# Attention's output normalisation split between ScalarE and VectorE, with the residual addition moved to the next turn

## What is computed

```python
x = x + 0.5 * ffn(layernorm(x))
x = x + attn(layernorm(x))
x = x + 0.5 * ffn(layernorm(x))

def attn(x):                       # windows of 128 tokens
    q, k, v = x @ Wq.T + bq, x @ Wk.T + bk, x @ Wv.T + bv
    scores = q @ k.T / sqrt(128)   # per window; only the 32 largest of each row are kept
    out = leaky_relu(softmax(top32(scores)) @ v, 0.01)
    r = out + x
    mu, var = mean(r), var(r)      # over the 128 features
    return (r - mu) / sqrt(var + 1e-5) * gamma + beta

def ffn(x):                        # router picks 2 of 8 experts per token, and a shared expert
    n = layernorm(x) * ln_gamma + ln_beta
    gates = softmax(top2(softmax(n @ router_w.T)))
    return sum(gate_e * swiglu_e(n)) + swiglu_shared(n)   # 384 wide per expert, 128 shared
```

## Time and profile before

| | us |
|---|---|
| median of 3 runs | 587.57 |
| lowest and highest | 584.46, 588.54 |
| the profiled execution | 590.26 |
| its span, first to last instruction | 588.5 |
| mean granted TensorE clock, share of full speed | 0.96 |

### The profile page before, as it was taken

One profiled execution on the slowest core, in us unless ns is written; L12 is line 12 of the kernel. 1 busy time (PEld: TensorE's weight loads), 2 busy tenths in 40 slices (PEclk: granted clock), 3 DMA queues, 4 the chain that ended last, 5 costly groups with the idle time before them and its releaser, 6 DMA issues.

```text
span 588.5 us, 14528 instructions
## 1 busy us (share of the span) xinstructions
PE 500.2 (85%) x3928; PEld 457.6 (78%) x3928; DVE 386.5 (66%) x1716; ACT 330.6 (56%) x792; POOL 332.8 (57%) x491
## 2 busy tenths in 40 slices
PE   2588999889999989998967399996899899899881
PEld 2466989889999989997964279784899889899780
DVE  5568774722558898877796978989885423222664
ACT  3376655665468576566753376763755446655330
POOL 2274856775566674365563506663667765565542
PEclk9999999999999999999987789996999999999986
DMA  6945787776776544783411174422658667777983
GB/s 180 319 105 177 229 239 247 225 244 228 257 258 235 195 171 160 248 283 123 156 43 58 42 250 159 167 99 98 219 202 233 239 219 245 258 257 235 321 274 110
DMA packets 88013, 117.83 MB, mean 200 GB/s; under 512 B 11848, under 2 KB 60880, under 8 KB 87936
## 3 DMA queue, kind: packets, MB, share of 16 engines
q1 hardware_dynamic: 76208, 96.75, 49.8%
q0 software_dynamic: 9312, 19.16, 9.4%
q10 hardware_dynamic: 2416, 0.99, 0.9%
HBM read 26.57 MB, written 26.19 MB: 90 GB/s over the span
## 4 chain that ended last, share of the span: by engine, by line
PE 51%; SPq 12%; ACT 11%; issue 8%; DVE 7%; DMA 7%; POOL 3%; ACTq 1%; POOLq 0%; DVEq 0%
PE ps_y L729 12%; PE ps_g L715 11%; PE ps_h L720 5%; PE ps_u L720 5%; SPq L440 4%; DMA xin<-rows 3%; SPq L483 3%; PE w L629 3%; SPq L478 3%; ACT zz L848 2%; PE ps_x L710 2%; PE w L659 2%; POOL rows L1552 2%; DMA yg<-results 2%; PE w L678 2%
## 5 line engine op out<-in xcount | busy, mean ns | idle before, releaser
L1569 POOL DMA_INDIRECT results<-raw_gu,idx x163 | 164.5, 1009 | 155.6 <-ACT raw_gu L928 112.8
L1552 POOL DMA_INDIRECT rows<-zz,s_idx x128 | 126.5, 988 | 65.0 <-issue 30.0
L729 PE MATMUL ps_y<-dn_t,raw_gu 128*128 x978 | 140.6, 281 | 10.2 <-ACT raw_gu L928 8.6
L715 PE MATMUL ps_g<-x_t,raw_dn 128*128 128x128 f32 x978 | 138.4, 278 | 0.0
L729 PEld LDWEIGHTS ps_y<-dn_t,raw_gu 128*128 128x128 f32 x978 | 124.3, 194 | 15.8 <-issue 15.4
L715 PEld LDWEIGHTS ps_g<-x_t,raw_dn 128*128 128x128 f32 x978 | 123.8, 194 | 3.0 <-issue 2.7
L928 ACT COPY raw_gu<-ps_y 128x128 f32<-128x128 f32 x163 | 43.0, 264 | 105.3 <-PE ps_y L729 104.1
L922 ACT ACTIVATE sil<-ps_g 128x384 f32<-128x384 f32 x163 | 80.1, 492 | 21.3 <-PE ps_g L715 20.1
L919 ACT ACTIVATE x_t<-ps_x,bf_c,gf_c 128x128 f32<-128x128 f32 x163 | 75.4, 463 | 18.3 <-PE ps_x L710 17.4
L1379 DVE TENSOR_TENSOR raw_gu<-sil,ps_u 128x384 f32<-128x384 f32 x82 | 45.1, 550 | 57.4 <-PE ps_u L720 45.2
L1379 DVE TENSOR_TENSOR raw_gu<-sil,ps_h 128x384 f32<-128x384 f32 x81 | 44.6, 551 | 50.8 <-PE ps_h L720 38.5
(11 more groups left out here) (168 smaller groups left out, 735.3 us busy)
## 6 DMA issues: line engine op xcount, KB each, us to landing
raw_dn<-gu_t SPq DMA_DIRECT2D x163, 384.0 KB
xin<-rows SPq DMA_DIRECT2D x163, 64.5 KB
yg<-results SPq DMA_DIRECT2D x15, 512.0 KB, 5.1
results<-raw_gu,idx POOLq DMA_INDIRECT x163
rows<-pads SPq DMA_DIRECT2D x40, 64.5 KB
rows<-pads SPq DMA_DIRECT2D x5, 451.5 KB, 6.0
rows<-zz,s_idx POOLq DMA_INDIRECT x128, 2.9
out<-xres SPq DMA_DIRECT2D x7, 256.0 KB, 2.8
```

Of the source, the lines that this page charges most:

```text
L715: t = pe.matmul(ps_g[k][:, c, :], ws[:, k4, c * P:(c + 1) * P], x_t[:, k, :], start=True, stop=True)
L729: t = pe.matmul(ps_y[:, 0, :], h_t[:, k4, c * P:(c + 1) * P], dn[:, bass.ds(off + c * D, D)], start=(c == 0), stop=(c == FC - 1))
L1552: pool.indirect_dma_start(xs, bass.IndirectOffsetOnAxis(s_idx[n][:, c, k:k + 1], 0), zz[n][:, k, c, :], None).then_inc(scat[n], 16)
L1569: pool.indirect_dma_start(yt, bass.IndirectOffsetOnAxis(idx[:, ky:ky + 1], 0), yb[:, ky, :], None).then_inc(yst[ky], 16)
```

## The change

ScalarE gets a new function `norm_r`: four activations per turn (one per tile) that write rn = rr * rstd + nmr, with rstd and nmr as per-partition pointers; it stands behind the exponentials in turns T1 to T7, and ahead of the shared Silu in T8. VectorE makes nmr for this normalisation with one more small `centre` at place 24. VectorE's `scaled` is removed, and `attended` becomes two operations on all four tiles at once, 128x512: rn = rn * gamma, and xres = xres + rn. They stand at the beginning of the next turn (T2 to T9), after the preparation of step p and in front of `stats_route`. A new buffer `rn` is added. The numbers in `WEAVE` are new.

```diff
@@ -112,22 +112,22 @@
 
 WEAVE = {
     "sp": """
...
     "pe": """
...
     "act": """
...
     "dve": """
...
     "pool": """
...
 }
 
 
@@ -282,6 +282,7 @@
         pr_t = sb("pr_t", [P, TB, P])
         o = sb("o", [P, TB, D])
         rr = sb("rr", [P, TB, D])
+        rn = sb("rn", [P, TB, D])
 
 
         gt = sb("gt", [P, NT, NE])
@@ -338,8 +339,8 @@
         s_ps, sc_sb, tk, nm_done, ex_done, pr_done, ri_done, prT_ps, prT_sb, o_ps = (
             sem(n) for n in ("s_ps", "sc_sb", "tk", "nm_done", "ex_done", "pr_done", "ri_done", "prT_ps", "prT_sb", "o_ps"))
         o_sb = sem("o_sb")
-        lr_done, rr_done, rg_done, xb_done, x2_done = (
-            sem(n) for n in ("lr_done", "rr_done", "rg_done", "xb_done", "x2_done"))
+        lr_done, rr_done, rn_done, rg_done, xb_done, x2_done = (
+            sem(n) for n in ("lr_done", "rr_done", "rn_done", "rg_done", "xb_done", "x2_done"))
         out_st, spare = sem("out_st"), sem("spare")
         passed = {e: sem(f"passed_{n}") for e, n in (
             (nc.vector.engine, "dve"), (nc.gpsimd.engine, "pool"), (nc.sync.engine, "sp"))}
@@ -353,7 +354,7 @@
 
         CREDITS = [(xT_ps, 4), (idx_cp, 4), (xT_sb, 3), (g_ps, 5), (u_ps, 4), (sil_done, 4), (h_done, 5),
                    (y_ps, 8), (y_sb, 6), (shh, 1), (xr_done, 1), (prT_sb, 1), (pr_done, TB), (ex_done, TB),
-                   (nm_done, 1), (o_ps, 1), (o_sb, 1), (v_sb, 1), (x2_done, TB), (cb, 2 * 3)]
+                   (nm_done, 1), (o_ps, 1), (o_sb, 1), (v_sb, 1), (x2_done, 1), (rn_done, TB), (cb, 2 * 3)]
 
         ctx.enter_context(nc.allow_low_precision(reason="rows' numbers are whole and below 2**24, exact in float32"))
         block = ctx.enter_context(nc.Block())
@@ -890,6 +891,14 @@
                 act.wait_ge(ex_done, (a + 1) * TB)
                 act.copy(sc[:], w0[:]).then_inc(sc_sb, 1)
 
+            def norm_r(A):
+
+                act.wait_ge(nw2, A * (N_NW + 1) + (N_NW + 1))
+                for k in range(TB):
+                    act.activation(rn[:, k, :], rr[:, k, :], ACT.Identity,
+                                   bias=nmr[:, AFTER_AT + k:AFTER_AT + k + 1], scale=rstd[:, AFTER_AT + k:AFTER_AT + k + 1]).then_inc(rn_done, 1)
+                    turn()
+
             def shared(R):
                 act.wait_ge(shG, R + 1)
                 act.activation(sg[:], w0[:].rearrange("p t d -> p (t d)"), ACT.Silu).then_inc(sg_done, 1)
@@ -992,11 +1001,15 @@
                     turn()
                     keys(p)
                     turn()
+                if a is None and A is not None:
+                    norm_r(A)
                 if J is not None:
                     shared(STEPS + J)
                     turn()
                 if a is not None:
                     exps(a)
+                if a is not None and A is not None:
+                    norm_r(A)
             gates_of_layer(1)
             turn.rest()
             for B in range(FIRST[-1], FIRST[-1] + YB):
@@ -1047,7 +1060,7 @@
                 stats(lambda k: rr[:, k, :], AFTER_AT, bn2, ag2, A * TB, turn)
 
             def stats_route(R, A, tile):
-                dve.wait_ge(x2_done, A * TB + 2 * TB)
+                dve.wait_ge(x2_done, A + 2)
                 stats(lambda k: res(tile, k), ROUTE_AT, bn3, ag3, R * TB, turn)
 
             def newton(n, chain, at, lo, mid, hi):
@@ -1088,7 +1101,12 @@
 
             def norms_after(n, A):
 
-                newton(n, nw2, A * N_NW, AFTER_AT, AFTER_AT + TB, AFTER_AT + TB)
+                if n == 0:
+                    dve.wait_ge(ag2, A * TB + TB)
+                if n < N_NORM:
+                    newton(n, nw2, A * (N_NW + 1), AFTER_AT, AFTER_AT + TB, AFTER_AT + TB)
+                else:
+                    centre(AFTER_AT, AFTER_AT + TB, nw2)
 
             def first_stats(R):
 
@@ -1315,21 +1333,16 @@
                 dve.tensor_tensor(xr, xr, wide(ba_b), ALU.add).then_inc(xb_done, 1)
                 turn()
 
-            def scaled(k, A):
-
-                if k == 0:
-                    dve.wait_ge(ag2, A * TB + TB)
-                dve.scalar_tensor_tensor(rr[:, k, :], rr[:, k, :], mv[:, AFTER_AT + k, 0:1], ga_b[:], ALU.subtract, ALU.mult).then_inc(rg_done, 1)
-                turn()
-
-            def attended(k, A):
-
-                dve.wait_ge(rg_done, A * TB + k + 1)
-                if k == 0:
-                    dve.wait_ge(nw2, A * N_NW + N_NW)
+            def attended(m, A):
+
+                if m == 0:
+                    dve.wait_ge(rn_done, A * TB + 2 * TB)
+                    dve.tensor_tensor(rn[:], rn[:], wide(ga_b), ALU.mult).then_inc(rg_done, 1)
+                else:
+                    dve.wait_ge(rg_done, A + 1)
                     dve.wait_ge(xb_done, A + 1)
-                dve.scalar_tensor_tensor(res(A * TB, k), rr[:, k, :], rstd[:, AFTER_AT + k:AFTER_AT + k + 1], res(A * TB, k),
-                                         ALU.mult, ALU.add).then_inc(x2_done, 1)
+                    xr = xres[:, A * TB:A * TB + TB, :]
+                    dve.tensor_tensor(xr, xr, rn[:], ALU.add).then_inc(x2_done, 1)
                 turn()
 
             def values(a):
@@ -1461,6 +1474,8 @@
                 R, rt = (None, None) if Jr is None else (STEPS + Jr, Jr * TB)
                 after = AFTER if a is not None else AFTER_LATE
                 if R is not None:
+                    attended(0, Jr)
+                    attended(1, Jr)
                     stats_route(R, Jr, rt)
                 if A is not None:
                     biased(A)
@@ -1475,12 +1490,8 @@
                         leaky(A, A % XRING)
                     if m == after + 1 and A is not None:
                         stats_after(A)
-                    if after + 2 <= m < after + 2 + TB and A is not None:
-                        scaled(m - (after + 2), A)
-                    if after + 2 <= m < after + 2 + N_NORM and A is not None:
+                    if after + 2 <= m <= after + 2 + N_NORM and A is not None:
                         norms_after(m - (after + 2), A)
-                    if after + 2 + N_NORM <= m < after + 2 + N_NORM + TB and A is not None:
-                        attended(m - (after + 2 + N_NORM), A)
                     if PICKS <= m <= PICKS + N_PICK and R is not None:
                         pick(m - PICKS, R, rt)
                     if m == (SHARED if a is not None else SHARED_LATE) and R is not None:
```

24 lines of the change are left out of this document (12 added, 12 removed).

## The result

| | before | after |
|---|---|---|
| median, us (runs) | 586.44 (4) | 592.98 (4) |
| lowest to highest, us | 584.46 to 588.54 | 590.36 to 596.97 |
| profiled execution, us (span) | 590.26 (588.5) | 591.35 (589.5) |

The account below looks back on a forecast made before the run. Bounds: VectorE's work from a turn's beginning to nmr in two holes, TensorE in full stretches. 0.8 + 1.1 + 1.2 - 0.6 - 0.6 = +1.9 us on 587.57 gives 589.5 us; 8-of-10 range 582.5 to 594.5.

Parts of the forecast that it names:

- The holes (T4, T5, T7: +0.8, +1.1, +1.2): Stretches 298 to 341 and 387 to 409.3 us, where TensorE lacks work: the pair in front of nmr lengthens them.
- The signs: nmr of T5 and T7 1 to 1.5 us later from s_idx; TensorE's idle time before L608 grows by as much.
- T8, T9 and the rest ... -0.6.: TensorE has blocks there, lacking 2.75 us in 440 to 480: -0.6 us, bounds -1.5 and +1.
- ScalarE. ... I take 0.: Four activations, 1.6 us per turn, nearly fit idle time behind T3's exponentials: 0, bounds 0 and +0.5 in seven turns.
- ScalarE delays the Silus: Rival, T1 to T7: rn's activations delay the first block work behind the exponentials; +5, above 594.5 us; chance 0.15.
- T6: ... -0.6: VectorE full from 344 to 387 us, 2.6 us less work there: -0.6 us, bounds -1.3 and 0.
- the full stretches give their saving: Rival: VectorE's freed time reaches the end in T2, T3, T6, T8; about -5, 582.5 us; chance 0.22.
- nothing measurable: Rival: moved block products cover the holes' extra, nothing else changes; 587.6 us; chance 0.15.
- The interleaving, taken as neutral: Block products in front of T7's nmr about the same in number, same blocks per turn in the new tables.
- the holes cost a clock step: Rival: more idle time prolongs TensorE's slow-clock stretches, +1.5 us per hole; 592.5 us; chance 0.13.
- Scatters beside the pair: T5: the pair falls between GpSimd's eight scatters, delaying block rows 0 to 0.7 us; one takes 1.3 us or more.

Follow-up runs that it names:

- dve_pair: The kernel before plus two VectorE operations of the new pair's shapes in front of stats_route, nothing removed: 592.55 us, ratio 1.0062, +3.7 us.
- order_alone_2: The kernel before with its old operations and the changed kernel's new interleaving, second measurement, on another chip: 592.19 us, ratio 1.0030, +1.8 us.
- eight_out: The kernel before without the eight scaled and attended instructions per turn, nothing in their place: 588.50 us, ratio 0.9984, -0.9 us.
- ops_old_order_2: The changed kernel's new operations with the old interleaving of before, second measurement, on another chip: 597.45 us, ratio 1.0137, +8.1 us against before.
- act_four: The kernel before plus ScalarE's four activations behind the exponentials in T1 to T8, nothing else changed: 593.50 us, ratio 1.0059, +3.5 us.
- beta_late: The kernel before with the addition of beta (biased) moved from in front of nmr to place 11, behind it: 590.20 us, ratio 1.0019, +1.1 us.

## Why the prediction was right, and where it fell short

- **The holes (T4, T5, T7: +0.8, +1.1, +1.2).** Right for the pair in the old interleaving, shown by dve_pair: +0.7, +1.4, +1.3. In the changed kernel only T5's is the pair's. T4's +0.9 and T7's +2.1 are there without the pair (order_alone_2: +0.9, +2.0), so that these two terms came near is in part luck. The signs: nmr of T5 came 1.43 us later from s_idx, as said; that of T7 came 2.1 us later, beyond the 1 to 1.5 given; TensorE's idle time before L609 in T7 grew by 1.85 us. T5's +1.1 was meant for TensorE, and at block 85's gate product it is +0.96. The moved transpose isn't the reason, since dve_pair, which leaves it in its place, has the same 20.39 us from s_idx to that product. Before, TensorE waited there for block 86's rows (0.23 us at 340.91), which it no longer does.
- **"T8, T9 and the rest ... -0.6."** Wrong. A stretch of T9 in which TensorE is full was taken as the picture of both turns. Their first halves have little cover: the pair lengthens them by 1.5 and 1.2 us (dve_pair), 2.7 us that stood nowhere in the sum. How much of it reaches the end isn't shown, nor is the -0.6.
- **"ScalarE. ... I take 0."** This is the term that was most mis-sized: +3.5 us (1.5 to 5.5) measured in the old interleaving. The reasoning by the engine's share of busy time and by one stretch of idle time behind T3's exponentials was right for the turns that it fits (T4 to T7 cost 0), but the cost sits in T3, T8 and T9, where xn, the probabilities' copy or zz is queued behind the four. Even the bound given, +0.5 in each of seven turns, is 3.5; that it would be uneven, with up to 3.1 in one turn, wasn't seen. No run has the four alone in the new interleaving, where T3's first half doesn't grow and T8's clock doesn't fall, so what they cost in the changed kernel stays open. The sentence that rn is ready some 5 us before it is needed failed in T2, where VectorE waited 1.40 us for it.
- **The rival "ScalarE delays the Silus".** Its engine was right and its size near (0.7 per turn in seven, about +5, against 3.5), its place wasn't: the Silus aren't what is late. It had a chance of 0.15 and its total, 594.5, is nearer to the 592.98 than the forecast's 589.5.
- **"T6: ... -0.6" and what removal is worth.** 15.7 us less work on VectorE bring 0.9 us (eight_out, at most 2.9 by its interval). The forecast's warning, that 2.1 us removed behind nmr don't pay for 1.4 added in front of it, is what happened, and it holds for the whole kernel. The rival "the full stretches give their saving" falls with it, and "nothing measurable" by the +4.8 and +6.8 us, whose intervals leave out zero.
- **The interleaving, taken as neutral.** It isn't, but its two effects nearly cancel: 6.4 us lost in first halves, 5 won in second ones, and the median +1.8 (not told from zero). Together with the operations it seems to give back some of their 8.1, by covering the pair in T4, T6 and T7: the changed kernel stands at +4.8 and +6.8 in its two measurements, with overlapping intervals. In its two profiles T2's s_idx comes 0.7 and 3.0 us earlier than before's, and 2.1 later in ops_old_order_2, so part of what is given back lies ahead of T3; which moved block does it wasn't tried.
- **The rival "the holes cost a clock step".** Not shown as a cost of the change: the long form of T5's second half came in act_four, eight_out and beta_late, and in neither profile of the changed kernel (17.8 and 17.7). In the old interleaving the new work did cost a clock step, but outside the holes, in T8 (act_four and ops_old_order_2, some 1.6 us).
- **Scatters beside the pair.** Right: 1.46 us beside 0.96. The Trainium skill, "GPSIMD Engine Reference", section "Key points", says that GpSimd contends with VectorE instructions that have two SBUF inputs, as both of the pair have. The trace agrees: 0.5 us more for one scatter, and 0.2 us on the way of all eight.

In sum: 1.9 us were forecast, for 3.1 of holes less 1.2 of gains elsewhere. In the old interleaving the holes came as forecast, the gains didn't, and ScalarE's 3.5 us and whatever reached the end of 2.7 on VectorE in T8 and T9 were missing. In the changed kernel the interleaving moves these costs about and covers a part; how its 4.8 us divide between pair, activations and interleaving isn't shown.

## What to carry to other kernels

Price an operation by its place, not by its engine's total: 15.7 us taken off VectorE behind the waiting point were worth 0.9 us, not told from zero, and 1.35 us per turn put in front of it cost 3.7 us (1.9 to 5.4). An engine that is busy 56% still delays others where its queue is in order; walk through every turn and ask what is queued directly behind the added work, since the cost sits in the two or three turns that differ from the one looked at. And when a wait of the profile changes its name after a reordering, compare the hole, not the name.

## What the runs showed of the hardware that was not expected

- **Another chip.** The kernel before took 586 to 591 us in three sets of runs and 650 us in one, on another chip, whose four profiles have 6 to 10% of the last chain released by something that the profile can't name. There the new interleaving was worst (1.0307), and on the next chip it can't be told from before (1.0030). The cause stays open; only ratios taken on the same chip were used.
- **A stretch with two lengths.** T5's second half takes 19 or 22 us with the same work, by how long TensorE is granted 1.2 GHz behind the hole (0.75 or 0.59 as the mean of 336 to 350 us). Over the 29 runs of before in the second set, time and mean granted clock go together (correlation -0.74, some 3.4 us less per 0.01 of clock, from 596.5 us at 0.943 to 584.9 at 0.967). A single profile can be off by that much in either direction, which is why the experiments were read by half turns.
- **An added 1.6 us that cost 3.1.** In T8 ScalarE's four activations delayed a product on TensorE. TensorE idled 2.14 us, its granted clock fell from 1.00 to 0.55 (423.8 to 425.8 us) and 0.50 (to 426.8), and the product and what came next ran at 1.2 GHz. So 1.5 us of queue brought another 1.6 us.
